# In the channel heads, GpSimd in place of VectorE adds the second mixture's two rows to x from batch 4 on

## The reference, cut to what matters

```python
# layer 2, mixture: every token takes two experts; y_i is the i-th expert's row for that token
x = x + g_ffn[2] * (w_0 * y_0 + w_1 * y_1 + shared experts)
# layer 3, attention over channels (8 heads of 16 channels), on the layer-normed x, with ctx as keys and values
n = _layernorm(x)
x = x + g_xattn[3] * gamma * attention(n, ctx)
# layer 3, mixture: layernorm, scores, the 4 best of 16 experts from the 2 best of 4 groups
```

## Time and profile before

| | us |
|---|---|
| three runs | 1308.42, 1308.56, 1309.82 |
| median | 1308.56 |
| the profiled execution, its own time | 1305.17 |
| its span (first to last instruction) | 1303.0 |
| busy: PE, DVE, ACT, POOL | 1089.4, 766.5, 494.2, 577.3 |
| `channel_heads`, first and last instruction of VectorE in it | 861.87 to 1088.0 |

### The profile page before, as it was taken

How to read it: one execution, slowest core, us unless ns; L and a number is a source line. 1 busy time by engine, 2 the same in 40 slices (tenths; PEclk the granted TensorE clock), 3 DMA queues, 4 the chain that set the end, 5 groups by cost and what they waited for, 6 DMA issues and landing times. The chain is left out here.

```text
span 1303.0 us, 25544 instructions
## 1 busy us (share of the span) xinstructions
PE 1089.4 (84%) x7222; PEld 799.5 (61%) x7223; DVE 766.5 (59%) x2814; ACT 494.2 (38%) x1309; POOL 577.3 (44%) x910
## 2 busy tenths in 40 slices
PE   4568799999999983999997999958887795799970
PEld 4355688877777761566655766634554554688860
DVE  6767443244444444687754655457888846555547
ACT  0046221223333320566563234414665532244430
POOL 5550027713333343555561524444333566455550
PEclk9998699999999995899998999977998966899995
DMA  9788962213333327111010234340000622366648
GB/s 399 212 259 280 340 218 108 107 57 110 106 106 106 106 86 314 50 52 64 2 38 22 98 87 134 122 157 1 2 2 2 242 82 84 114 164 164 164 120 320
DMA packets 92301, 169.45 MB, mean 130 GB/s; under 512 B 11102, under 2 KB 70750, under 8 KB 91230
## 3 DMA queue, kind: packets, MB, share of 16 engines
q1 hardware_dynamic: 72393, 107.63, 27.1%
q0 software_dynamic: 17664, 48.91, 10.4%
q10 hardware_dynamic: 2160, 11.86, 2.2%
HBM read 82.75 MB, written 85.61 MB: 129 GB/s over the span
## 5 line engine op out<-in xcount | busy, mean ns | idle before, releaser
L2177 PE MATMUL bank<-weights,xT 128*128 x832 | 240.8, 412 | 0.2 <-ACT xT L2271 0.2
L1999 POOL DMA_INDIRECT slots_out<-weights,y_rows x128 | 122.8, 959 | 134.8 <-DVE y_rows L2443 89.6
L2177 PEld LDWEIGHTS bank<-weights,xT 128*128 128x128 f32 x832 | 142.5, 191 | 24.6 <-issue 0.7
L1993 POOL DMA_INDIRECT slots_in<-xn_wide,row_in x106 | 102.4, 966 | 101.3 <-DMA slots_in<-xs_wide 49.8
L1999 POOL DMA_INDIRECT slots_out<-pack,y_rows x80 | 76.7, 959 | 142.8 <-DVE y_rows L2443 135.3
L2271 ACT COPY xT<-bank 128x256 f32<-128x256 f32 x208 | 77.4, 372 | 116.9 <-PE bank L2169 116.5
L1412 PE MATMUL bank<-ctx,weights 32*128 32x256 f32 x512 | 79.6, 451 | 33.0 <-DVE weights L1566 26.9
L2088 PE MATMUL bank<-xT,weights 128*128 128x256 f32 x416 | 104.5, 396 | 2.3 <-ACT xT L2235 2.3
L1485 ACT ACTIVATE weights<-bank 128x512 f32<-128x512 f32 x128 | 72.6, 596 | 72.0 <-PE bank L1420 72.0
L2420 DVE TENSOR_TENSOR weights<-weights,bank 128x128 f32<-128x128 f32 x128 | 36.8, 288 | 102.4 <-ACT weights L2275 102.4
L1566 DVE TENSOR_REDUCE weights<-bank 128x2 f32<-128x512 f32 x128 | 85.6, 681 | 10.3 <-PE bank L1412 9.8
(11 more groups left out here) (428 smaller groups left out, 2456.4 us busy)
## 6 DMA issues: line engine op xcount, KB each, us to landing
slots_in<-xs_wide SPq DMA_DIRECT2D x16, 2112.0 KB, 19.0
weights<-slots_in SPq DMA_DIRECT2D x96, 132.0 KB, 2.3
xs_wide<-slots_in SPq DMA_DIRECT2D x72, 132.0 KB, 2.3
weights<-slots_out SPq DMA_DIRECT2D x17, 512.0 KB, 11.5
rows<-slots_out SPq DMA_DIRECT2D x16, 512.0 KB, 3.3
weights<-in_l_gu SPq DMA_DIRECT2D x1, 7040.0 KB
pack<-slots_in SPq DMA_DIRECT2D x40, 132.0 KB, 2.1
weights<-in_l_gu ACTq DMA_DIRECT2D x1, 4608.0 KB, 14.4
```

The costliest lines, as they stand in the source:

```text
L1993: pool.indirect_dma_start(out=slots_in, in_=xn_wide[:, t, :], in_offset=None, out_offset=bass.IndirectOffsetOnAxis(ap=row_in[:, t, i:i + 1 ...
L1999: pool.indirect_dma_start(out=slots_out, in_=y[:, n % U, :], in_offset=None, out_offset=bass.IndirectOffsetOnAxis(ap=y_rows[:, n % U:n % U ...
L2177: last = nc.tensor.matmul(out, xT[:, n.c % 2, c, :], flat(gu_w[:, ds(e, 1), c, :]), start=(c == 0), stop=(c == C - 1 and layer != 2))
```

## The change

From batch 4 on (`POOLED = 4`) the two rows are scaled and added by GpSimd. Where VectorE had two scalar_tensor_tensor per batch, GpSimd has four instructions: two tensor_scalar that multiply the rows in place by their weights, and two tensor_tensor that add them to x. They stand in GpSimd's list behind `head_factors(b + 3)` and ahead of `keys(b + 1)`, in passes 0 to 11. VectorE's bn_stats of that batch (n = 4) now waits for the second sum of GpSimd; two semaphores, `scaled` and `summed`, are new. SyncE's load of the experts waits for the last sum on GpSimd in place of VectorE's last join. `OWN_ROOTS` stays at 13.

```diff
             def join_place(k, i):
-                return 2 * i + k + 1 if k < 2 else 4 * k + i + 1
+                if k < 2:
+                    return 2 * i + k + 1
+                return 4 * k + i + 1 if k < POOLED else 4 * POOLED + 2 * (k - POOLED) + i - 1
...
-                sp.wait_ge(joined, join_place(NB - 1, 1))
+                sp.wait_ge(summed, 2 * (NB - POOLED))
                 load_experts(sp, 3)
...
+                def head_join(k):
+                    at = 2 * (k - POOLED)
+                    pool.wait_ge(rows_in[sum(k >= t0 for t0, _ in loads) - 1], 16)
+                    pool.wait_ge(b_added, 8)
+                    for i in range(2):
+                        nc.gpsimd.tensor_scalar(pairs_of[:, k, i, :], pairs_of[:, k, i, :], weight[:, k, i:i + 1], 1.0,
+                                                ALU.mult, ALU.mult).then_inc(scaled, 1)
+                    for i in range(2):
+                        pool.wait_ge(scaled, at + i + 1)
+                        if i:
+                            pool.wait_ge(summed, at + 1)
+                        nc.gpsimd.tensor_tensor(x[:, k, :], x[:, k, :], pairs_of[:, k, i, :], ALU.add).then_inc(summed, 1)
...
                     if b + 3 < NB:
                         head_factors(b + 3)
+                    if POOLED <= b + 4 < NB:
+                        head_join(b + 4)
...
                     if i == 0:
                         dve.wait_ge(b_added, 2 if k < 2 else 8)
                         dve.wait_ge(rows_in[sum(k >= t0 for t0, _ in loads) - 1], 16)
+                    elif k >= POOLED and i == 2:
+                        dve.wait_ge(summed, 2 * (k - POOLED + 1))
...
-                    if 2 <= b + 4 < NB and n in (2, 3, 4, 5, 7):
+                    if 2 <= b + 4 < NB and n in ((2, 3, 4, 5, 7) if b + 4 < POOLED else (4, 5, 7)):
                         join(b + 4, (2, 3, 4, 5, 7).index(n))
```

More of the change, by code:

```diff
@@ L1169, in channel_heads @@
              rooted, r_normed, r_turned, rx_ready, l_ready, l_taken, tri_ready, marked, sel_ready, counted, cnt_copied,
-             route_own, placed, pool_own, padded, c_turned, c_copied, bias_ready, b_added, joined, head_var, late_own,
+             route_own, placed, pool_own, padded, c_turned, c_copied, bias_ready, b_added, joined, scaled, summed, head_var, late_own,
              late_rooted) = (
@@ L1174, in channel_heads @@
                                  "rx", "l", "ltaken", "tri", "marked", "sel", "counted", "cntc", "rown", "placed",
-                                 "pown", "padded", "ct", "cc", "bias", "ba", "joined", "hvar", "lown",
+                                 "pown", "padded", "ct", "cc", "bias", "ba", "joined", "scaled", "summed", "hvar", "lown",
                                  "lrooted"))
@@ L1207, in channel_heads @@
             LEAD = SB + TB
+            POOLED = 4
             def join_place(k, i):
-                return 2 * i + k + 1 if k < 2 else 4 * k + i + 1
+                if k < 2:
+                    return 2 * i + k + 1
+                return 4 * k + i + 1 if k < POOLED else 4 * POOLED + 2 * (k - POOLED) + i - 1
             def score_bank(s):
```

## The result

| | before | after |
|---|---|---|
| runs beside each other, median | 1308.49 (1307.88 to 1309.82, 4 runs) | 1300.05 (1298.91 to 1300.65, 4 runs) |
| profiled execution, its own time | 1305.17 | 1298.91 |
| its span, mean granted clock | 1303.0, 0.918 | 1297.2, 0.923 |

The ratio is 0.9933, with a 95% interval of 0.9916 to 0.9950: 8.4 us faster, where 2.6 were forecast. The steps of the prediction on the steady passes came out to the hundredth; what it left without a size decided this result. Four later timings of the same changed kernel gave 0.9993, 0.9989, 0.9987 and 0.9981. The experiments show in which pass the first differs from them; why it does is not settled.

A forecast was written before the change was run, and what follows sets the result against it. No engine is full: a ring of waits through VectorE, TensorE and ScalarE sets the 10.23 us steady pass. -2.8 (steady passes) - 1.7 (passes 9 to 11) + 1.9 (hindrance) = -2.6, so 1308.56 becomes 1306.0, range 1303.6 to 1309.8.

The forecast's parts named there:

- The first row instruction is worth nothing, the second 0.35 in a pass: Steady passes: without the first, VectorE just waits longer for TensorE; without the second, step 5's peaks start earlier, 0.25 to 0.40.
- 8 x 0.35 = 2.8: Gain in us over passes 1 to 8 from the second row instruction leaving VectorE; range 2.0 to 3.2.
- GpSimd's work is hidden; L1648 is not held up: GpSimd's four added instructions, 2.65 us a pass, fit its idle time at price 0; a one-element VectorE instruction keeps 0.14.
- The slower rival: L1648 is held up by GpSimd's burst in every pass, about +4.3 us, 1312.9; chance 0.12, late roots included.
- meets nothing: The experts' load starts some 6 us earlier and, at 16% mean DMA share there, does not move the end.
- 2.65 here against 0.94 there: Us per pass for the row work on GpSimd against VectorE, agreeing with the skill's rule that GpSimd is about twice as slow.
- 4 x 0.40 = 1.6: Gain in us from both row instructions in passes 9 and 11; with 0.1 for pass 10, 1.7 together (0.8 to 2.0).
- 0.9 + 0.3 + 0.7 = 1.9: Loss in us in passes 9, 10 and 11, as VectorE's routing instructions wait beside GpSimd's longer burst; 1.0 to 2.9.
- forecast +0.2: Passes 9 to 11: the 1.7 us gained from the row instructions set against 1.9 us lost to the engines' mutual hindrance.
- The rest, clock of TensorE in the late passes above all, to both sides: Chance left over after the forecast and three rivals, put on either side of the range, without a size in us.
- A sum of -2.6: The forecast's total change in us: -2.8 steady passes, -1.7 passes 9 to 11, +1.9 hindrance; forecast's chance 0.50.

The follow-up runs named there:

- late_load: Changed kernel with SyncE's load of the experts' weights held until the last variance of the heads' loop is written; 1305.65 us in one run.
- after_c: The changed kernel again, nothing altered, on a chip at clock 0.917; 1305.89 us against 1308.25 for the kernel before, ratio 0.9987.
- after_again: The changed kernel again, nothing altered, on a slower chip at clock 0.887; 1423.17 us against 1424.01 for the kernel before, ratio 0.9993.

## Why the prediction was wrong, by its own steps

- **The first row instruction is worth nothing, the second 0.35 in a pass**: right, by the idle time that was named; 0.36 was measured, and each was confirmed alone. Passes 2 to 8 gave 2.51. "8 x 0.35 = 2.8" counted pass 1 as well, and rightly: from its first peaks to those of pass 2 it went from 9.96 to 9.57 on the slower kind, and from 10.44 to 9.95 in the first pair of profiles. Together 2.9.
- **GpSimd's work is hidden; L1648 is not held up**: right (roots 1.4 us early, L1669 0.14). The slower rival falls with it. The load of the experts "meets nothing": right, by late_load. The "2.65 here against 0.94 there" set four instructions against two; one by one an add took 0.80 on GpSimd and the multiplication with its addition 0.47 on VectorE.
- **Passes 9 to 11, "4 x 0.40 = 1.6"**: mis-sized. 1.0 was measured, nearly all in pass 9. In pass 11 VectorE is busy, but the idle 0.55 for TensorE's scores stands behind the rows and takes their gain, the same mechanism that I had read for step 3 of a steady pass and did not look for here.
- **The hindrance, "0.9 + 0.3 + 0.7 = 1.9"**: real, and mis-sized: 0.66 + 0 + 0.10 = 0.8. L1702 waited for one GpSimd instruction and not for two, L1760 for none, L1791 lost 0.1. I had taken the middle between bounds for an overlap that the order of the work allowed but did not force. (The bounds of the three passes add up to 1.2 to 2.95, not "1.0 to 2.9".) The two errors cancel, by luck: net -0.2 (the first pair of profiles: -0.1), forecast +0.2.
- **"The rest, clock of TensorE in the late passes above all, to both sides"**: the step that failed. It was named and got neither a size nor a place in the range. In pass 15 the rows at either clock differ by 4.7 to 4.9 us, in pass 10 by 1.0, in pass 14 by 0.8, in pass 16 by up to 1.6. Before's pass 15 stood in its trace with 14.83 of 15.60 busy at 0.52, so several us were there to be gained by anything that gave it the full clock. Whether the gain of 2.9 upstream did so is not shown: after_c has the same gain at the same times, and its pass 15 is long. A sum of -2.6 with a possible -4.7 behind it would have reached down to about 1301, and to 1300 with pass 10.

So the mechanism of the change was right, and its own worth is 2.9 + 0.2 = 3.1 us by the passes, which lies within the interval of each of the four later timings. The first timing had that and a short pass 15. It is shown that pass 15 is short or long by TensorE's clock on this kind of chip, and that a mere shift in time can bring the short case; what decides in which executions it comes is open.

## What to carry to other kernels

Look through the trace, also far behind the change, for stretches in which TensorE alone is busy at the half clock, and put their price on the range: a change of a few us upstream, even a pure delay, can bring or take it. A gain of under 1% of such a kernel is worth what repeats on another chip; compare passes at the same clock, not totals. GpSimd took this work for nothing where it fitted its idle time and VectorE's instructions beside it were peaks on banks, statistics and single elements (passes 1 to 8); tensor_scalar and tensor_tensor in SBUF beside it cost 0.66 us in pass 9. So where the data are early, place such work in stages of the first kind.

## What the runs showed that I had not expected

- The chips are of two kinds for this kernel: mean clock 0.91 to 0.92 and 1306 to 1308 us, or 0.88 to 0.89 and 1424 to 1425 (three chips of each). Pass 12 takes 9.72 in the one at a clock of 1.00, and 13.01 in the other at 0.97 (13.03 at 1.00 in after_again); pass 15 takes 15.6 and 23.2, both at 0.50 to 0.52, and 23.16 at 0.60 in after_again. So on the slower kind the granted clock is not what sets these passes. Windows of the kernel before on the slower kind, passes 12 and 15, and under them rows of ScalarE's timeline there:

```profile
1108.94:1121.95 13.01, 10.19 (x128) 6.36 (x126) 7.33 (x17) 6.89 (x15) 9.03 (x14) 0.97 0.83 334
1151.70:1174.87 23.17, 14.27 (x82) 7.69 (x82) 4.87 (x31) 5.88 (x12) 8.64 (x9) 0.50 0.16 59
```

```profile
1118.48 0.60 ACT L1485 ACTIVATE weights<-bank 128x512 f32<-128x512 f32 x1 [2.57 <-DMA ctx<-in_ctx]
...
1156.23 0.60 ACT L1485 ACTIVATE weights<-bank 128x512 f32<-128x512 f32 x1 [4.56 <-issue]
...
1165.57 0.18 ACT L1496 ACTIVATE pack<-bank 128x16 f32<-128x16 f32 x1 [5.24 <-remote]
```

  In passes 12 and 15 on the faster kind ScalarE waits for TensorE alone. Here it stands idle for 2.57 us in pass 12, put down to a DMA, and for 4.56 and 5.24 in pass 15, put down to no instruction of the core. The cause is open.
- On the faster kind pass 15 is short (10.7 to 10.95) or long (15.6 to 15.7) in the eleven profiles; nothing between was seen.
